# Neighbourhood attention block on one core: the MLP's chain moved over two steps of the band loop, with another order of PSUM bank owners

## The chip, the cores and the metric
One core of one Trainium2 chip. The metric is the device time of one execution, in microseconds (us), median of three runs. Five engines work in parallel, each on its own queue of instructions in program order, and wait for one another through semaphores: TensorE (PE: matrix products into PSUM), VectorE (DVE), ScalarE (ACT), GpSimd (POOL, which works on SBUF alone here) and SyncE (SP, which issues all the DMAs here).

## The reference
The input x is 16 images of 64 x 64 positions with 256 channels, in float32. In short:

```
def norm(x, w, b): return w * arcsinh(x) + b
q, k, v = split(norm(x, n1_w, n1_b) @ qkv_w + qkv_b)        # 8 heads of 32
attn = softmax over the 3 x 3 neighbourhood of (q * 32**-0.5) . k   # clipped at the image's edges
h   = x + (attn . v) @ proj_w + proj_b
out = h + gelu(norm(h, n2_w, n2_b) @ mlp_w1 + mlp_b1) @ mlp_w2 + mlp_b2     # 512 hidden, exact gelu
```

## The kernel before, in words
**Bands.** The image rows are cut into 128 bands (`BANDS`) of 8 rows, 512 tokens each. A band is 8 tiles of 8 x 8 queries, and each tile looks at a 10 x 10 window of keys; rows of marks, added to queries and keys, rule out keys outside the 3 x 3 neighbourhood. Channels lie on partitions. Every product is made in float16 parts: an operand is split in a high part (a rounding, `_hi`) and a low part (the rest, `_lo`), and `three` issues three matmuls, hi x hi, hi x lo and lo x hi. ScalarE mostly makes the high part out of PSUM, VectorE the low part; for the probabilities, the normalised input (`a_parts`), the MLP's input (`b_parts`) and the gelu's output (`g_parts`) GpSimd makes the low part.

**Steps and slots.** The loop runs over steps t = 0 to 129. A step has `SLOTS` = 4 slots k of two tiles, and each engine's `step` function writes out by hand what it issues in which slot. The order of the work is this order; the semaphores only hold it back. On TensorE a slot is: `subtract_max` of its two tiles, `scores` of the next slot, a first product group, `weighted` of the first tile (probabilities x values), a second product group, `weighted` of the second tile, `scores_t` of the next slot's two tiles. In step t the attention is that of band t. The product groups of step t in the kernel before are: slot 0 `turn` (transposes of the second half of band t-1's output), k of band t+2, then the projection of t-1; slot 1 q and v of t+2; slot 2 `mlp_out` of t-2 and `turn` of the first half of t; slot 3 `mlp_in` of t-1.

**Around them.** arcsinh is done as square, log, exp (`root`) and log on ScalarE with `magnitude`, `sum` and `sign` on VectorE: chain 1 for the input of band t+3, chain 2 for h of band t-1. ScalarE's `gelus` loads another activation table before its four gelus and the old one after them (lines 993 and 999). VectorE also takes the maximum of the scores, divides by the sum (`sum_reciprocal`, `normalise`, lines 803 and 812), makes h (`h_from_projection`, 751), adds a bias (`h_plus_bias`, 783) and makes y (`result`, 790).

**PSUM.** Banks 3 to 7 belong to attention (scores 3 and 4, transposed scores 5 and 6, weighted values 7). Banks 0 to 2 are shared by all the products, by the lists at the top (`TURN_BANK`, `K_BANK`, `PROJ_BANK`, `Q_BANK`, `V_BANK`, `OUT_BANK`, `IN_BANK`); before a product overwrites a bank, TensorE waits for the last reader of that bank. `weighted` uses bank 7 for every tile, so it waits for `normalise` of the tile before. In `mlp_in` the first product (bank 2) waits for both y of the band before.

**SyncE.** In step t it issues: `place_queries` (12 copies and the mask's) and `place_keys` (12 copies) for band t+1, SBUF to SBUF; `load_x` of t+4; `store_v` of t+2, which writes the values to a DRAM buffer `v_rows` when both `v_low` are done (2 DMAs); `store_y` of t-2, half 0; `gather_v` of band t+1 (8 DMAs out of `v_rows`, which need the store of t+2 to have landed, since windows reach one row into the next band); `store_y`, half 1.

Lines in the rows: 369 is every TensorE matmul (the helper `mm`), 446 the turns; 989 and 990 the exponentials, 997 the gelu, 911, 915, 920, 929 and 938 the arcsinh chain on ScalarE, 975 `v_high`; 713 the sum, 717 the sign, 771 `v_low`; 1072 p_lo, 1087 and 1089 `b_parts`, 1096 and 1098 `g_parts`; 306 `place_keys`, 314 `store_v`, 325 `gather_v`, 330 `store_y`.

Of the kernel before, what the change touches and what calls it, by code (L numbers as in the profile page):

```python
# [48 lines left out]
XT = 5  # L49
# [11 lines left out]
PROJ_BANK = [0, 1]  # L61
Q_BANK = [2, 0]
V_BANK = [1, 2]
# [39 lines left out]
def build(nc, x, qkv_w, qkv_b, proj_w, proj_b, n1_w, n1_b, n2_w, n2_b, mlp_w1, mlp_b1, mlp_w2, mlp_b2,  # L103
# [3 lines left out]
    with ExitStack() as ctx:  # L107
# [146 lines left out]
        def _(sp):  # L254
# [112 lines left out]
        def _(pe):  # L367
# [11 lines left out]
            def k_product(t, g):  # L379

                if g == 0:
                    pe.wait_ge(a_lo_ready, signals(t, G, G))
                if has(t - 4):
                    pe.wait_ge(gelu_ready, signals(t - 4, MT, 3 + g))
                elif g == 0:
                    pe.wait_ge(v_lo_ready, signals(t - 1, 2, 1))
                    pe.wait_ge(o_lo_ready, signals(t - 3, 2, 1))
                else:
                    pe.wait_ge(v_lo_ready, signals(t - 1, 2, 2))
                k_matmuls(g)  # L390
# [7 lines left out]
            def q_product(t, g):  # L398

                if g == 0:  # L400
                    pe.wait_ge(k_lo_ready, signals(t, G, 2))
                elif has(t - 3):
                    pe.wait_ge(h_ready, signals(t - 3, G, 1))
                else:
                    pe.wait_ge(q_lo_ready, signals(t - 1, G, 2))
# [9 lines left out]
            def v_product(t, n):  # L415

                if n == 1:
                    pe.wait_ge(q_lo_ready, signals(t, G, 1))
                elif has(t - 3):
                    pe.wait_ge(h_ready, signals(t - 3, G, 2))  # L420
# [11 lines left out]
            def turn(t, half):  # L432

                pe.wait_ge(norm_ready, signals(t, TILES, TILES // 2 * (half + 1)))
                if half == 0:
                    if has(t + 2):
                        pe.wait_ge(v_lo_ready, signals(t + 2, 2, 1))
                    else:
                        pe.wait_ge(h_ready, signals(t - 1, G, 2))
                elif has(t - 1):  # L440
                    pe.wait_ge(gelu_ready, signals(t - 1, MT, 2))
# [8 lines left out]
            def projection(t, par, g):  # L450
# [5 lines left out]
                elif has(t - 1):  # L456
                    pe.wait_ge(gelu_ready, signals(t - 1, MT, 3))
# [6 lines left out]
            def mlp_in(t, m):  # L464

                if m == 0 and has(t - 1):
                    pe.wait_ge(y_ready, signals(t - 1, 2, 2))
                elif m == 0:
                    pe.wait_ge(v_lo_ready, signals(t + 3, 2, 2))
                elif m == 1 and has(t - 1):  # L470
                    pe.wait_ge(y_ready, signals(t - 1, 2, 1))
                elif m == 1:
                    pe.wait_ge(q_lo_ready, signals(t + 3, G, 2))
                elif m == 2 and has(t + 1):
                    pe.wait_ge(o_lo_ready, signals(t + 1, 2, 1))
                elif m == 2:
                    pe.wait_ge(h_ready, signals(t, G, 2))
                else:
                    pe.wait_ge(gelu_ready, signals(t, MT, 1))
# [7 lines left out]
            def mlp_out(t, g):  # L487

                if g == 0:
                    pe.wait_ge(g_lo_ready, signals(t, MT, MT))  # L490
                    if has(t + 4):
                        pe.wait_ge(q_lo_ready, signals(t + 4, G, 2))
                    elif has(t + 1):
                        pe.wait_ge(h_ready, signals(t + 1, G, 1))
                    else:
                        pe.wait_ge(gelu_ready, signals(t, MT, 2))
                elif has(t + 4):
                    pe.wait_ge(v_lo_ready, signals(t + 4, 2, 2))
                else:
                    pe.wait_ge(gelu_ready, signals(t, MT, 4))  # L500
                for m in range(MT):
                    s = three(ps[:, OUT_BANK[g], :], [w[:, m, g * P:(g + 1) * P] for w in (w2_hi, w2_lo)],
# [76 lines left out]
            def opening(t):  # L579
# [3 lines left out]
                if t > -3:  # L583
                    pe.wait_ge(a_lo_ready, signals(t + 2, G, G))
                    if t == -1:
                        pe.wait_ge(v_lo_ready, signals(0, 2, 1))
                    k_matmuls(0)
                    if t == -1:
                        pe.wait_ge(v_lo_ready, signals(0, 2, 2))
                    k_matmuls(1)  # L590
                    pe.wait_ge(k_lo_ready, signals(t + 2, G, 2))
                    q_matmuls(0)
                    if t == -1:
                        pe.wait_ge(q_lo_ready, signals(0, G, 2))
                    q_matmuls(1)
                    v_matmuls(0)
                    pe.wait_ge(q_lo_ready, signals(t + 2, G, 1))
                    v_matmuls(1)
# [6 lines left out]
            def step(t, u):  # L605
                par = t % 2
                att, pre, post, fin, fill = has(t), has(t + 2), has(t - 1), has(t - 2), has(t + 3)
                for k in range(SLOTS):
# [28 lines left out]
                    if k == 1 and pre:  # L637
                        v_product(t + 2, 0)
                    if k == 1 and pre:
                        v_product(t + 2, 1)  # L640
                    if k == 2 and fin:
                        mlp_out(t - 2, 1)
                    if k == 2 and att:
                        turn(t, 0)
                    if k == 3 and post:
                        mlp_in(t - 1, 2)
                        mlp_in(t - 1, 3)
# [14 lines left out]
        def _(v):  # L662
# [153 lines left out]
            def opening(t):  # L816
# [10 lines left out]
                else:  # L827
# [5 lines left out]
                    sum1_(t + 3)  # L833
                    q_low(t + 2, t % 2, 0)
                    q_low(t + 2, t % 2, 1)
                    sign1(t + 3, t + 3)
                    v_low(t + 2, 0)
                    v_low(t + 2, 1)
# [3 lines left out]
            def step(t, u):  # L842
                par, old = t % 2, 1 - t % 2
                att, pre, post, fin, fill = has(t), has(t + 2), has(t - 1), has(t - 2), has(t + 3)
                for k in range(SLOTS):
                    ta, ka = (t, k + 1) if k + 1 < SLOTS else (t + 1, 0)
                    more = has(ta)
                    if more:
# [6 lines left out]
                    if k == 1 and pre:  # L855
                        q_low(t + 2, par, 0)
                    if k == 2 and post:
                        sign2(t - 1, old)
                    if k == 2 and fill:
                        magnitude1(t + 3, (u + 3) % XT)  # L860
                    if k == 3 and att:
                        o_low(t, par, 0)
                    if k == 3 and fill:
                        sign1(t + 3, (u + 3) % XT)
                    if k == 3 and post:
                        h_plus_bias(t - 1, old)
# [5 lines left out]
                    if k == 0 and pre:  # L872
                        k_low(t + 2, 1)
# [3 lines left out]
                    if k == 1 and pre:  # L877
                        q_low(t + 2, par, 1)
                    if k == 1 and post:
                        sum2_(t - 1)  # L880
                    if k == 1 and pre:
                        v_low(t + 2, 0)
                    if k == 2 and fill:
                        sum1_(t + 3)
                    if k == 2 and fin:
                        result(t - 2, par, 0)

# [3 lines left out]
                    if k == 0 and post:  # L891
                        magnitude2(t - 1, old)
                    if k == 1 and pre:
                        v_low(t + 2, 1)
                    if k == 2 and fin:
                        result(t - 2, par, 1)
# [9 lines left out]
        def _(act):  # L906
# [94 lines left out]
            def opening(t):  # L1001
# [6 lines left out]
                else:  # L1008
# [5 lines left out]
                    log1_(t + 3)  # L1014
                    q_high(t + 2, t % 2, 0)
# [3 lines left out]
                    v_high(t + 2, 0)  # L1019
                    v_high(t + 2, 1)  # L1020

            def step(t, u):
                par, old = t % 2, 1 - t % 2
                att, pre, post, fill = has(t), has(t + 2), has(t - 1), has(t + 3)
                for k in range(SLOTS):
# [4 lines left out]
                    if k == 2 and post:  # L1030
                        log2_(t - 1)
# [4 lines left out]
                    if k == 0 and pre:  # L1036
                        k_high(t + 2, 0)
                        k_high(t + 2, 1)
                        windows_main(t + 2, par, 0)
                        windows_main(t + 2, par, 1)  # L1040
                    if k == 1 and pre:
                        q_high(t + 2, par, 0)
                    if k == 1 and post:
                        square2(t - 1, old)
                    if k == 1 and pre:
                        q_high(t + 2, par, 1)
                    if k == 1 and post:
                        log_of_square(ln2_s[:], sq2, ln2a, t - 1)
                        root(ln2_s[:], ln2a, root2, t - 1)
                    if k == 1 and pre:  # L1050
                        v_high(t + 2, 0)
                        v_high(t + 2, 1)
                    if k == 2 and fill:
# [3 lines left out]
                        log1_(t + 3)  # L1057
                    if k == 3 and post:
                        gelus(t - 1)
# [7 lines left out]
        def _(pool):  # L1067
# [56 lines left out]
            def step(t, u):  # L1124
                par, old = t % 2, 1 - t % 2
                att, pre, post, fin, fill = has(t), has(t + 2), has(t - 1), has(t - 2), has(t + 3)
                for k in range(SLOTS):
# [3 lines left out]
                    if k == 0 and fin:  # L1131
                        g_parts(t - 2, (0, 1))
# [35 lines left out]
```

## Time and profile before
| | |
|---|---|
| time, median of 3 runs | 4478.32 us (4474.22 to 4479.34) |
| profiled execution | 4478.71 us, span 4476.9 us |
| busy: PE / DVE / ACT / POOL | 4089.1 (91%) / 3570.1 (80%) / 3663.0 (82%) / 3539.3 (79%) |
| PE waits for y of `result` (DVE L790) | 283.3 us in 126 waits |
| mean granted TensorE clock | 0.969 of full speed |
| DMA engines busy | about half the time, 134 GB/s |

A busy PE is not a PE at its peak: matmuls overlap, and the start of one to the start of the next tells the pace. Waits are put down to the work that released them. The clock is granted at one of two levels, so a mean of 0.969 means short stretches at half speed.

### The profile page before, as it was taken

To read this page: it belongs to the slowest core of one execution; us is meant where nothing else is said; L and a number is where in the kernel's file an instruction comes from. 1 tells how busy PE (TensorE), PEld (TensorE's weight loads), DVE (VectorE), ACT (ScalarE), POOL (GpSimd) and SP (SyncE) were. 2 spreads that over 40 slices of the span, in tenths; PEclk is the share of its full clock that TensorE was granted. 3 is DMA by queue.
4 is the path that set the end of the run, shared out by engine and by line. 5 is a ranking of instruction groups with operands and counts; after the bars stand their busy time and mean duration, and the time that the engine had idled before them with its cause. 6 is when DMAs were issued, how large, how long until landed. Compare 5 with 4: busy or idle time off the path is not lost.

```text
span 4476.9 us, 123492 instructions
## 1 busy us (share of the span) xinstructions
PE 4089.1 (91%) x47688; PEld 2566.3 (57%) x47688; DVE 3570.1 (80%) x6174; ACT 3663.0 (82%) x5377; POOL 3539.3 (79%) x4092
## 2 busy tenths in 40 slices
PE   5999999999999999999999999999999999999997
PEld 3555555555555555555555555555555555555553
DVE  5788788888878888887888888788878888887884
ACT  4888888888888888888888888888888888888884
POOL 2788888887888888888878888888888788788885
PEclk8999999999999999999999999999999999999998
DMA  4555555555555555555555555555555555555551
GB/s 121 129 142 134 136 135 138 138 134 137 138 135 134 141 137 132 142 134 138 133 140 138 133 136 139 136 133 142 133 137 135 138 138 133 137 138 136 134 133 55
DMA packets 511560, 598.82 MB, mean 134 GB/s; under 512 B 76798, under 2 KB 409600, under 8 KB 508416
## 3 DMA queue, kind: packets, MB, share of 16 engines
q1 hardware_dynamic: 510976, 590.93, 51.2%
q8 instruction: 379, 6.21, 0.6%
q14 instruction: 205, 1.68, 0.1%
HBM read 197.30 MB, written 135.40 MB: 74 GB/s over the span
## 4 chain that ended last, share of the span: by engine, by line
PE 51%; DVE 23%; issue 14%; ACT 10%; POOL 1%; SPq 1%; DMA 0%; DVEq 0%; POOLq 0%; ACTq 0%
PE ps L369 49%; DVE ln_u L717 4%; DVE y L790 4%; DVE v_nat L771 4%; DVE o_norm L812 3%; DVE ln_u L713 3%; ACT ln_s L920 3%; ACT ln_s L911 3%; ACT ln_s L915 3%; DVE ln_u L710 2%; ACT q_nat L944 2%; PE ps L446 2%; DVE maxima L796 2%; DVE recip L803 1%; POOL g_lo L1098 0%
## 5 line engine op out<-in xcount | busy, mean ns | idle before, releaser
L1072 POOL TENSOR_TENSOR p_lo<-prob,p_hi 100x512 f16<-100x512 f32 x1024 | 1312.7, 1287 | 623.7 <-ACT p_hi L990 623.5
L369 PE MATMUL ps<-b_hi,w_hi 128*128 128x512 f16 x1024 | 435.7, 425 | 288.4 <-DVE y L790 283.3
L989 ACT ACTIVATE prob<-ps 100x512 f32<-100x512 f32 x1024 | 610.2, 596 | 80.2 <-PE ps L369 54.9
L713 DVE TENSOR_TENSOR ln_u<-ln_u,ln_s 128x1024 f32<-128x1024 f32 x256 | 531.0, 2074 | 147.2 <-ACT ln_s L920 143.4
L812 DVE TENSOR_TENSOR o_norm<-ps,recip 64x128 f32<-64x128 f32 x2048 | 591.7, 289 | 49.4
L1098 POOL TENSOR_TENSOR g_lo<-g,g_hi 128x512 f16<-128x512 f32 x512 | 594.9, 1162 | 41.0
L369 PEld LDWEIGHTS ps<-v_win,p_hi 100*128 100x128 f16 x8192 | 474.7, 98 | 261.3 <-DVE o_norm L812 70.7
L990 ACT ACTIVATE p_hi<-ps 100x512 f16<-100x512 f32 x1024 | 613.7, 599 | 0.0
L796 DVE TENSOR_REDUCE maxima<-ps 128x8 bf16<-128x800 f32 x512 | 504.6, 986 | 88.3 <-PE ps L369 84.2
L369 PE MATMUL ps<-v_win,p_hi 100*128 100x65 f16 x8192 | 517.5, 194 | 47.7 <-DVE o_norm L812 26.4
L997 ACT ACTIVATE g<-ps,b 128x512 f32<-128x512 f32 x512 | 344.6, 686 | 254.5 <-PE ps L369 253.6
L369 PE MATMUL ps<-v_win,p_lo 100*128 100x65 f16 x4096 | 481.6, 192 | 0.0
L1087 POOL CAST b_hi<-ln_u 128x512 f16<-128x512 f32 x256 | 329.3, 1286 | 150.2 <-DVE ln_u L717 150.2
L369 PE MATMUL ps<-b_lo,w_hi 128*128 128x512 f16 x1024 | 432.4, 422 | 0.0
L369 PE MATMUL ps<-b_hi,w_lo 128*128 128x512 f16 x1024 | 421.2, 411 | 0.0
L929 ACT ACTIVATE ln_s<-ln_u 128x1024 f32<-128x1024 f32 x128 | 135.3, 1057 | 332.4 <-DVE ln_u L713 332.4
L369 PE MATMUL ps<-a_hi,wqkv_hi 128*128 128x512 f16 x1024 | 391.8, 383 | 13.3 <-DVE bp L705 6.3
L369 PE MATMUL ps<-g_hi,w_hi 128*128 128x512 f16 x1024 | 392.4, 383 | 8.3 <-POOL g_lo L1098 8.3
L966 ACT ACTIVATE k_win<-k_nat 128x640 f16<-128x640 f16 x512 | 349.4, 730 | 51.7 <-DVE k_nat L764 47.7
L369 PE MATMUL ps<-g_lo,w_hi 128*128 128x512 f16 x1024 | 390.6, 381 | 0.0
L369 PE MATMUL ps<-g_hi,w_lo 128*128 128x512 f16 x1024 | 390.4, 381 | 0.0
L369 PE MATMUL ps<-a_lo,wqkv_hi 128*128 128x512 f16 x1024 | 390.3, 381 | 0.0
(91 smaller groups left out, 10887.7 us busy)
## 6 DMA issues: line engine op xcount, KB each, us to landing
keys<-k_win SPq DMA_DIRECT2D x1536, 100.0 KB, 2.2
v_win<-v_rows SPq DMA_DIRECT2D x1024, 101.6 KB
queries<-q_nat SPq DMA_DIRECT2D x1536, 64.0 KB
v_rows<-v_nat SPq DMA_DIRECT2D x256, 260.0 KB, 5.4
xT<-in_x_dram SPq DMA_DIRECT2D x128, 512.0 KB, 4.3
out_dram<-y SPq DMA_DIRECT2D x256, 256.0 KB, 2.7
queries<-in_query_mask_dram SPq DMA_DIRECT2D x128, 160.0 KB
keys<-in_mlp_w_dram SPq DMA_DIRECT2D x2, 512.0 KB, 7.7
```

The source lines that it names most:

```text
L369: return pe.matmul(o, a, b, start=start, stop=stop, skip_group_check=True)
L713: v.tensor_tensor(u, u, root, ALU.add).then_inc(s, 1)
L717: v.scalar_tensor_tensor(out=out.bitcast(U32), in0=sign_of.bitcast(U32), scalar=SIGN, in1=log.bitcast(U32), op0=ALU.bitwise_and, op1=ALU.b ...
L796: v.tensor_reduce(maxima[k % 2][:].rearrange("p n a -> p (n a)"), ps[:, B_S:B_S + 2, 0:PAIRS * NK].rearrange("p n (a k) -> p n a k", k=NK) ...
L812: s = v.tensor_tensor(o_norm[r, c], av[r, :, HD * e:HD * e + HD], recip[c % 2][r].to_broadcast([NQ, PAIRS, HD]), ALU.mult)
L966: s = act.activation(to[:, :, 1:1 + TS], rows, ACT.Copy)
L989: act.activation(prob[b][0:NK], ps[0:NK, B_ST + b, :], ACT.Exp, scale=INV * INV).then_inc(prob_ready, 1)
L990: act.activation(p_hi[b][0:NK], ps[0:NK, B_ST + b, :], ACT.Exp, scale=INV * INV).then_inc(p_hi_ready, 1)
L997: act.activation(g32[:, m, :], ps[:, IN_BANK[m], :], ACT.Gelu, bias=b1[:, m:m + 1], scale=INV).then_inc(gelu_ready, 1)
L1072: pool.tensor_tensor(p_lo[b][0:NK], prob[b][0:NK], p_hi[b][0:NK], ALU.subtract).then_inc(p_lo_ready, 1)
L1087: pool.tensor_copy(b_hi[:, g, :], ln2_u[:, g * TOK:(g + 1) * TOK]).then_inc(b_hi_ready, 1)
L1098: pool.tensor_tensor(g_lo[:, m, :], g32[:, m, :], g_hi[:, m, :], ALU.subtract).then_inc(g_lo_ready, 1)
```

## The change
The MLP's first product moves from the last slot of one step to slot 1 of the next, so that in step t both `mlp_in` and `mlp_out` are those of band t-2; with it move `sign2`, `b_parts`, `gelus` and `h_plus_bias`. q and v change slots (both in slot 2, v first), `mlp_out` goes to slot 3, and V's banks become 0 and 1. The square and the roots of both arcsinh chains are placed anew. On SyncE `store_y` of half 0 goes behind `gather_v`. `mlp_out` waits for the four parts of g one by one. The same instructions are issued per band. The core of the diff:

```
-V_BANK = [1, 2]
+V_BANK = [0, 1]
@@ SyncE step
-                if has(t - 2):
-                    store_y(t - 2, 0)
                 if has(t + 1):
                     gather_v(t + 1, 1 - par)
                 if has(t - 2):
+                    store_y(t - 2, 0)
                     store_y(t - 2, 1)
@@ TensorE: k_product
                 if g == 0:
                     pe.wait_ge(a_lo_ready, signals(t, G, G))
-                if has(t - 4):
-                    pe.wait_ge(gelu_ready, signals(t - 4, MT, 3 + g))
...
+                    if has(t - 3):
+                        pe.wait_ge(o_lo_ready, signals(t - 3, 2, 1))
...
+                elif has(t - 5):
+                    pe.wait_ge(y_ready, signals(t - 5, 2, 2))
@@ q_product
-                if g == 0:
-                    pe.wait_ge(k_lo_ready, signals(t, G, 2))
-                elif has(t - 3):
-                    pe.wait_ge(h_ready, signals(t - 3, G, 1))
+                if g == 1:
+                    pe.wait_ge(v_lo_ready, signals(t, 2, 1))
+                elif has(t - 4):
+                    pe.wait_ge(gelu_ready, signals(t - 4, MT, 4))
@@ v_product
-                if n == 1:
-                    pe.wait_ge(q_lo_ready, signals(t, G, 1))
+                if has(t - 4):
+                    pe.wait_ge(gelu_ready, signals(t - 4, MT, 2 + n))
@@ turn
-                        pe.wait_ge(v_lo_ready, signals(t + 2, 2, 1))
+                        pe.wait_ge(v_lo_ready, signals(t + 2, 2, 2))
...
-                elif has(t - 1):
-                    pe.wait_ge(gelu_ready, signals(t - 1, MT, 2))
+                elif has(t - 2):
+                    pe.wait_ge(y_ready, signals(t - 2, 2, 1))
@@ mlp_in
-                if m == 0 and has(t - 1):
-                    pe.wait_ge(y_ready, signals(t - 1, 2, 2))
...
+                if m == 0:
+                    if has(t + 4):
+                        pe.wait_ge(k_lo_ready, signals(t + 4, G, 2))
...
+                elif m == 3:
+                    pe.wait_ge(gelu_ready, signals(t, MT, 1))
+                elif has(t + 1):
+                    pe.wait_ge(h_ready, signals(t + 1, G, m))
@@ mlp_out
-                if g == 0:
-                    pe.wait_ge(g_lo_ready, signals(t, MT, MT))
...
                 for m in range(MT):
+                    if g == 0:
+                        pe.wait_ge(g_lo_ready, signals(t, MT, m + 1))
@@ TensorE step, first product groups (before weighted of tile 2k)
-                    if k == 1 and pre:
-                        q_product(t + 2, 0)
-                        q_product(t + 2, 1)
-                    if k == 2 and fin:
+                    if k == 1 and fin:
+                        mlp_in(t - 2, 0)
+                        mlp_in(t - 2, 1)
+                    if k == 2 and pre:
+                        v_product(t + 2, 0)
+                        v_product(t + 2, 1)
+                    if k == 3 and fin:
                         mlp_out(t - 2, 0)
-                    if k == 3 and post:
-                        mlp_in(t - 1, 0)
-                        mlp_in(t - 1, 1)
@@ second groups: mlp_in 2 and 3 in slot 1, q 0 and 1 in slot 2, mlp_out 1 in slot 3
@@ VectorE: h_from_projection
+                if g == 0 and has(t - 2):
+                    v.wait_ge(y_ready, signals(t - 2, 2, 2))
@@ GpSimd: a_parts, step
-                pool.wait_ge(pe_v, signals(t - 1, 2, 2))
+                pool.wait_ge(pe_q, signals(t - 1, G, G))
...
                     if k == 0 and fin:
-                        g_parts(t - 2, (0, 1))
+                        b_parts(t - 2)
...
                     if k == 1 and fin:
+                        g_parts(t - 2, (0, 1))
+                    if k == 2 and fin:
                         g_parts(t - 2, (2, 3))
-                    if k == 2 and post:
-                        b_parts(t - 1)
```

The steps of VectorE and ScalarE after the change, slot by slot (rn is `sum_reciprocal` and `normalise` of a tile, pp the two exponentials of a tile):

```
VectorE  k=0: sign2(t-2), maximum, o_low(t-1,1), k_low x2, rn, magnitude1(t+3), h_from_projection x2, rn
         k=1: maximum, sum1_(t+3), magnitude2(t-1), rn, h_plus_bias(t-2), rn
         k=2: maximum, sign1(t+3), v_low x2, rn, q_low x2, rn
         k=3: maximum, o_low(t,0), sum2_(t-1), rn, result(t-2) x2, rn
ScalarE  k=0: pp, o_high(t-1,1), pp, k_high x2, square1, log, root of t+3
         k=1: pp, pp, gelus(t-2)
         k=2: pp, log1_(t+3), pp, v_high x2, square2(t-1), q_high x2, log of the square
         k=3: pp, o_high(t,0), pp, root of t-1, windows_main x2 (t+2), log2_(t-1)
```

## Rows read from the trace of the kernel before

**Rows 1.** The profile's page, part 1: busy time and share of each engine.
```profile
PE 4089.1 (91%) x47688; PEld 2566.3 (57%) x47688; DVE 3570.1 (80%) x6174; ACT 3663.0 (82%) x5377; POOL 3539.3 (79%) x4092
```

**Rows 2.** Waits of TensorE, whole run: total us, times, longest.
```profile
PE ps L369 <- DVE y L790: 283.3, 126, 2.3
...
PE ps L369 <- DVE o_norm L812: 26.4, 126, 3.2
```

**Rows 3.** Timeline of TensorE, two bands: start, us, work, [idle before].
```profile
2249.32 0.61 PE L369 MATMUL ps<-b_hi,w_hi 128*128 128x512 f16 x1 [2.29 <-DVE y L790]
...
2257.35 0.61 PE L369 MATMUL ps<-minus_ident,maxima 128*128 128x128 bf16 x8
...
2261.45 0.23 PE L369 MATMUL ps<-v_win,p_hi 100*128 100x65 f16 x2
...
2265.24 0.61 PE L369 MATMUL ps<-minus_ident,maxima 128*128 128x128 bf16 x8
...
2268.86 0.23 PE L369 MATMUL ps<-v_win,p_hi 100*128 100x65 f16 x2
...
2271.86 0.23 PE L369 MATMUL ps<-v_win,p_hi 100*128 100x65 f16 x2
...
2272.69 0.61 PE L369 MATMUL ps<-minus_ident,maxima 128*128 128x128 bf16 x8
...
2284.27 0.39 PE L369 MATMUL ps<-b_hi,w_hi 128*128 128x512 f16 x1 [2.29 <-DVE y L790]
...
2317.59 0.61 PE L369 MATMUL ps<-b_hi,w_hi 128*128 128x512 f16 x1 [2.29 <-DVE y L790]
```

**Rows 4.** Table by windows: clock behind the wait at 2249.32.
```profile
2249.32:2252.73 3.41, 3.40 (x9) 1.23 (x10) 3.41 (x4) 3.16 (x5) 3.10 (x2) 0.51 0.41 104
```

**Rows 5.** Timeline of ScalarE: table load, exponentials, `v_high`.
```profile
2257.41 1.28 ACT L999 ACT_TABLE_LOAD   x1
...
2271.92 1.07 ACT L975 ACTIVATE v_nat<-ps 128x512 f16<-128x512 f32 x2
...
2275.28 0.58 ACT L989 ACTIVATE prob<-ps 100x512 f32<-100x512 f32 x1
...
2276.23 1.06 ACT L911 ACTIVATE ln_s<-xT 128x1024 f32<-128x1024 f32 x1
```

**Rows 6.** Groups by line: the costs of VectorE's and GpSimd's steps.
```profile
L713 DVE TENSOR_TENSOR ln_u<-ln_u,ln_s 128x1024 f32<-128x1024 f32 x256 | 531.0, 2074 | 147.2 <-ACT ln_s L920 143.4
...
L1072 POOL TENSOR_TENSOR p_lo<-prob,p_hi 100x512 f16<-100x512 f32 x1024 | 1312.7, 1287 | 623.7 <-ACT p_hi L990 623.5
...
L1087 POOL CAST b_hi<-ln_u 128x512 f16<-128x512 f32 x256 | 329.3, 1286 | 150.2 <-DVE ln_u L717 150.2
...
L771 DVE SCALAR_TENSOR_TENSOR v_nat<-ps,v_nat 128x512 f16<-128x512 f32 x256 | 175.6, 687 | 6.5 <-ACT v_nat L975 2.6
```

**Rows 7.** Timeline of SyncE's queue in the opening steps: gather, store.
```profile
70.30 6.46 SPq L325 DMA_DIRECT2D v_win<-v_rows  x8
...
95.19 0.98 SPq L314 DMA_DIRECT2D v_rows<-v_nat  x2
...
101.22 6.42 SPq L325 DMA_DIRECT2D v_win<-v_rows  x8
...
131.41 6.41 SPq L325 DMA_DIRECT2D v_win<-v_rows  x8
```

**Rows 8.** Timeline of SyncE's queue, steady state: `store_y`, `gather_v`.
```profile
2316.12 0.35 SPq L330 DMA_DIRECT2D out_dram<-y  x1
...
2316.58 6.77 SPq L325 DMA_DIRECT2D v_win<-v_rows  x8
```

**Rows 9.** Timeline of TensorE, opening: `weighted` released by the gather at 70.30.
```profile
79.16 0.29 PE L369 MATMUL ps<-v_win,p_hi 100*128 100x65 f16 x2 [5.03 <-DMA v_win<-v_rows]
```

**Rows 10.** The page, part 6: DMA issues, KB, us to landing.
```profile
v_rows<-v_nat SPq DMA_DIRECT2D x256, 260.0 KB, 5.4
...
out_dram<-y SPq DMA_DIRECT2D x256, 256.0 KB, 2.7
```

More of the change, by code:

```diff
@@ L636, in step @@
                         projection(t - 1, 1 - par, 1)
[L637 to L642, printed above, removed]
+                    if k == 1 and fin:
+                        mlp_in(t - 2, 2)
+                        mlp_in(t - 2, 3)
+                    if k == 2 and pre:
+                        q_product(t + 2, 0)
+                        q_product(t + 2, 1)
                     if k == 2 and att:
                         turn(t, 0)
[L645 to L647 removed]
+                    if k == 3 and fin:
+                        mlp_out(t - 2, 1)
                     if att:
@@ L847, in step @@
                     more = has(ta)
+                    if k == 0 and fin:
+                        sign2(t - 2, par)
                     if more:
@@ L854, in step @@
                         k_low(t + 2, 0)
-                    if k == 1 and pre:
-                        q_low(t + 2, par, 0)
-                    if k == 2 and post:
-                        sign2(t - 1, old)
+                        k_low(t + 2, 1)
+                    if k == 1 and fill:
+                        sum1_(t + 3)
+                    if k == 1 and post:
+                        magnitude2(t - 1, old)
                     if k == 2 and fill:
-                        magnitude1(t + 3, (u + 3) % XT)
+                        sign1(t + 3, (u + 3) % XT)
+                    if k == 2 and pre:
+                        v_low(t + 2, 0)
+                        v_low(t + 2, 1)
                     if k == 3 and att:
                         o_low(t, par, 0)
-                    if k == 3 and fill:
-                        sign1(t + 3, (u + 3) % XT)
                     if k == 3 and post:
-                        h_plus_bias(t - 1, old)
+                        sum2_(t - 1)
                     if att:
@@ L876, in step @@
                         h_from_projection(t - 1, old, (u - 1) % XT, 1)
-                    if k == 1 and pre:
+                    if k == 1 and fin:
+                        h_plus_bias(t - 2, par)
+                    if k == 2 and pre:
+                        q_low(t + 2, par, 0)
                         q_low(t + 2, par, 1)
[L879 to L885, printed above, removed]
+                    if k == 3 and fin:
                         result(t - 2, par, 0)
+                        result(t - 2, par, 1)
                     if att:
@@ L890, in step @@
                         normalise(t, 2 * k + 1)
[L891 to L896, printed above, removed]
             for t_ in queries:
@@ L1038, in step @@
                         k_high(t + 2, 1)
[L1039 to L1053, printed above, removed]
+                    if k == 0 and fill:
                         square1(t + 3, (u + 3) % XT)
@@ L1056, in step @@
                         root(ln1_s[:], ln1a, root1, t + 3)
-                        log1_(t + 3)
-                    if k == 3 and post:
-                        gelus(t - 1)
+                    if k == 1 and fin:
+                        gelus(t - 2)
+                    if k == 2 and pre:
+                        v_high(t + 2, 0)
+                        v_high(t + 2, 1)
+                    if k == 2 and post:
+                        square2(t - 1, old)
+                    if k == 2 and pre:
+                        q_high(t + 2, par, 0)
+                        q_high(t + 2, par, 1)
+                    if k == 2 and post:
+                        log_of_square(ln2_s[:], sq2, ln2a, t - 1)
+                    if k == 3 and post:
+                        root(ln2_s[:], ln2a, root2, t - 1)
+                    if k == 3 and pre:
+                        windows_main(t + 2, par, 0)
+                        windows_main(t + 2, par, 1)
+                    if k == 3 and post:
+                        log2_(t - 1)
             for t in range(-3, 0):
```

82 lines of the change are left out of this document (34 added, 48 removed).

## The prediction
> **What bounds the kernel now.** I read the page's busy times first [rows 1]: TensorE 91%, the other three engines about 80%. Divided by 128 bands that is 27.9 us a band for VectorE, 28.6 for ScalarE and 27.7 for GpSimd. The band's length stands in TensorE's timeline [rows 3]: the product `mlp_in` starts after the same wait at 2249.32, 2284.27 and 2317.59, so two bands are 68.27 us and one is 34.13. Three engines thus have 5.5 to 6.5 us to spare, and TensorE is the one to follow. Its waits [rows 2] are of one kind: 126 times on `result` (y), 283.3 us in all or 2.25 a band, and 126 times on `normalise` (o_norm), 0.2 a band. A second loss goes with the first: matmuls last 0.61 us after the wait at 2249.32 and at 2317.59, but 0.39 after that at 2284.27 [rows 3], and the granted clock of the 3.41 us behind the first is 0.51 of full speed, its 1.2 GHz level [rows 4]. The band with that stretch is 34.95 us, the one without it 33.32, so the level costs 1.6 us in every other band, 0.8 a band. What TensorE did ahead of each fall was to wait 2.29 us; after one such wait of two it did not fall.
>
> TensorE without either loss: 33.32 - 2.25 - 0.2 = 30.87 us a band. That is the floor. Its slots [rows 3], counted from `subtract_max` of slot 0 at 2257.35 as s0: s1 = s0 + 7.89, s2 = s0 + 15.34. `weighted` of the first tile of slot 0 comes at s0 + 4.10, of another slot at s + 3.62 (2268.86), of the second tile at s + 6.62 (2271.86). The four products of each slot have the same length after the change, as each slot still holds two groups of 12 passes of 512 columns (or 24 of 256), and the turns stay in slots 0 and 2, so these offsets can be kept.
>
> **What goes.** `mlp_in`'s first product waited for both results of the band before, because banks 2 and 0 were OUT banks until `result` had read them. It now comes in slot 1, and `result` in slot 3, so between `mlp_out` and the next owners of its banks (k's second product and the turn, slot 0) lies the end of a step. I cost the y wait at 0 and its slow stretches at 0. No matmul, activation, copy or DMA is added or taken away in a steady band; only the order changes, so the question is what is late next. I went round each engine's queue at the floor's offsets.
>
> **ScalarE and TensorE, slot 2.** The gelus move to slot 1. Before, the table load behind the last gelu runs from 2257.41 to 2258.69, s0 + 1.34 [rows 5]; after `mlp_in`'s last product at the same place of slot 1 this gives s2 + 1.34. A pair of exponentials takes 0.95 (2275.28 to 2276.23), GpSimd's p_lo 1.29 on the mean [rows 6], and `weighted` can start at s2 + 3.7 with the latencies, against 3.62: a stall of 0.1 (in slot 0 the turn hid this). From there ScalarE does the pair (0.95), log1 (128x1024 like the square at 2276.23, 1.06, the next start 1.0 later), a second pair (0.95) and two `v_high` (1.07), then VectorE the second `v_low`, 0.69 [rows 5, 6]: 1.34 + 0.95 + 1.0 + 0.95 + 1.07 + 0.1 + 0.69 = s2 + 6.1 to 6.3. I take 6.2. q's second product, whose bank 0 is now v's first, waits for the first `v_low` at about s2 + 5.6 where it would start at 5.3 to 5.4: 0.2.
>
> **VectorE, slot 3.** `root2` stands behind all four exponentials and `o_high`, so it ends near s3 + 0.6 + 0.95 + 0.5 + 0.95 + 1.07 = 4.1; `sum2_` needs it and lasts 2.07 [rows 6], to 6.2; reciprocal and `normalise` of the slot's first tile stand behind it, to 7.0. `weighted` of the slot's second tile wants that bank at 6.62: 0.4 to 0.5. With 0.1 and 0.2 of slot 2, TensorE alone would run a band in 30.87 + 0.8 = 31.6 us. If `sum2_` or ScalarE were half a us faster there, the third stall would go and it would be 31.2.
>
> **GpSimd.** `b_parts` moves to slot 0, behind two p_lo and VectorE's `sign2`, which now opens the step. Casts of b average 1.29 us, a subtraction like p_lo 1.29 at most [rows 6]; with some overlap two of each are about 4.9, from about s0 + 4.7 to 9.6, against need at s1 + 1.0 for the first half (ready by then, as it is half of the work) and s1 + 1.7 = s0 + 9.6 for the second. Cost 0, up to 0.3 if the casts stay slow. Behind it stand `windows_bottom` and then p_lo of slot 1, whose `weighted` has about 0.2 of slack; same bounds. `h_plus_bias`, `magnitude2` and the a parts keep over 0.5 us of slack in their slots. The new wait of `h_from_projection` for y of two bands back is for something done a slot earlier: 0.
>
> **SyncE's queue.** This is what I think decides. `store_v` waits for `v_low` of both halves, which moves from slot 1 and 2 to s2 + 6.2; before, the store left at 2276.6, s2 + 4, and SyncE then waited for y with time over. `gather_v` waits until that store has landed, and `weighted` of the next step's slot 0 waits for the gather. The chain [rows 7 to 9]: from the store's start at 95.19 to the gather's at 101.22 are 6.03 us, when nothing but the landing was between; from a gather's start at 70.30 to the `weighted` released by it at 79.16 are 8.86 us. Together 14.89. From there TensorE needs 2272.69 - 2261.45 = 11.24 us to the start of slot 2, and 6.2 to `v_low`. The circle closes in 14.89 + 11.24 + 6.2 = 32.3 us, over TensorE's 31.6. `store_y` of half 0 moves behind the gather, which keeps y out of this circle; its issue is 0.35 us [rows 8].
>
> SyncE's queue by itself is a circle too. Gather to gather in the opening steps, without y stores, is 131.41 - 101.22 = 30.19 us [rows 7]; two y stores with gaps (0.35 and about 0.5) make 31.1, and the steady state's longer issues (a gather 6.77 in row 8 against 6.46 in rows 7) some 31.3 to 31.7.
>
> The landing is the unknown term. The v store shows 5.4 us, behind the x load issued just before it, a y store of the same 256 KB that stands alone 2.7 [rows 10]. If the 5.4 is the queue behind x, then SyncE's wait for `v_low` (0.6 us at a band of 32.3) is taken off it, and the circle is 31.7; if not, 32.3. At the row of y it would be 29.6 and bind nothing. I take 32.1, near the upper end, as x is still directly in front.
>
> The Trainium skill (DMA: Bandwidth & Descriptors, "Anatomy of one DMA", the SWDGE path) says that a DMA's fixed cost is about 2.0 us, most of it the wait until the last byte is confirmed, and that the rest is bytes over 436 GB/s. For 260 KB this would be an estimated 2.6 us, near the y row's 2.7 and half of the store's 5.4; by that rule the chain through the store is no bound, and the time is that of rival A.
>
> **Sum.** The wait is met 126 times, so 126 x (34.13 - 32.1) = 256 us go. The ends: the last band's MLP now runs wholly in the last step behind its arsinh, while its gelus of the band before precede it on ScalarE; `mlp_out` starts as soon as the first quarter of g is split. I put +3 us (bounds -5 and +10). Profiled time 4478.7 - 256 + 3 = 4226. The median of the runs before is 4478.3, the same.
>
> **Rivals.**
> A: the store lands sooner, and TensorE's small stalls or SyncE's issue circle set the band at 31.2 to 31.7. For it: the y row's 2.7 us; against: x in front. 126 x 2.6 = 330 us less: 4150. Chance 0.22.
> B: the clock still falls in every other band, now after the waits at `weighted` and in slot 3. For it: the level fell after 2.29 us of waiting; against: each new wait is under 1 us. Price 0.8 a band: 4330. Chance 0.15.
> C: a wait of the same 2 us replaces the old one, GpSimd's chain in slot 0 and 1 being a microsecond later than I have it: no change, 4475 or so. Against it: 6.4 us of spare time a band there. With other partial losses between 4370 and 4470, chance 0.10.
> D, slower: the wait for `v_win` drops the clock each band rather than each second one. Everything from `weighted` in slot 0 to slot 2 is on the circle, so a 3.4 us stretch at half speed adds 1.7 us to 32.3, and two in a row 3.4: 35.7 a band, 4478.7 + 126 x 1.57 = 4677. It turns to slower once the clock costs more than 2.0 us a band. Against: it cost 0.8 with a wait of 2.3. Chance 0.06.
>
> **Chances and range.** Forecast, 4190 to 4290: 0.47. The range takes in A and B: 4130 to 4370. No change within 0.2% (9 us, about what a measurement here can tell) is a small part of C, 0.03; slower is D with a little of C, 0.08; faster 0.89.
>
> **What would show it.** Right: no wait on y; a band of 32.1; TensorE waiting 0.3 to 1 us on v_win once a band, 0.1 to 0.5 on o_norm in slot 3; `store_v` directly behind `v_low` with SyncE idle before it; hardly any half clock. Wrong: v_win not in the waits (A); PEclk still near 0.97 (B); a wait over 1 us on p_lo or b_lo (C). A store that lands after about 5.4 us again confirms that term; one near 3 breaks it.

## The result, and the profile after

The changed kernel takes 4221.46 us (median of 4 runs, 4218.82 to 4228.25) against 4478.4 us; the ratio is 0.943 with a 95% interval of 0.9414 to 0.9447. The forecast was 4226. The profiled execution took 4228.25 us, its span is 4226.5.

The page of the changed kernel, parts 1 and 4 (the chain that ended last, by engine and by line; TensorE's line is now 368):

```profile
PE 4022.6 (95%) x47688; PEld 2518.8 (60%) x47688; DVE 3637.2 (86%) x6174; ACT 3630.9 (86%) x5377; POOL 3636.9 (86%) x4092
...
PE 46%; SPq 18%; DMA 14%; POOL 9%; issue 7%; ACT 4%; DVE 2%; POOLq 0%; ACTq 0%; DVEq 0%
PE ps L368 46%; SPq L325 14%; DMA v_win<-v_rows 8%; DMA v_rows<-v_nat 6%; POOL p_lo L1065 3%; POOL g_lo L1091 2%; SPq L306 2%; DVE v_nat L766 1%; SPq L292 1%; POOL g_hi L1089 1%; POOL a_lo L1073 1%; ACT ln_s L920 1%; POOL a_hi L1071 1%; ACT p_hi L981 1%; ACT v_nat L966 1%
```

TensorE is busy 95% of the span, and the chain that ended last now runs through SyncE's issues (SPq 18%) and through DMAs in flight (14%). The same line of the kernel before:

```profile
PE 51%; DVE 23%; issue 14%; ACT 10%; POOL 1%; SPq 1%; DMA 0%; DVEq 0%; POOLq 0%; ACTq 0%
```

TensorE's waits over the whole run (total us, times, longest) answer to [rows 2]:

```profile
PE ps L368 <- DMA v_win<-v_rows: 114.3, 109, 5.7
PE ps L368 <- POOL p_lo L1065: 25.5, 25, 2.7
...
PE ps L368 <- DVE o_norm L807: 7.8, 6, 2.7
```

The wait on y (283.3 us in 126 times) is gone altogether, and 114.3 us on v_win, 0.9 a band, stand in its place. The wait on o_norm in slot 3, forecast at 0.4 to 0.5 us a band, isn't there: 7.8 us in 6 waits, all outside the steady part.

The band's length is read from SyncE's queue (start, us, work): a gather near the loop's start and the 124th after it (the first row shows two of its eight DMAs),

```profile
133.36 1.69 SPq L325 DMA_DIRECT2D v_win<-v_rows  x2
...
4113.28 6.44 SPq L325 DMA_DIRECT2D v_win<-v_rows  x8
```

3979.92 us for 124 bands, 32.10 us each; the forecast was 32.1. The kernel before, from 131.41 [rows 7] to this gather, has 34.12 over as many:

```profile
4362.10 6.44 SPq L325 DMA_DIRECT2D v_win<-v_rows  x8
```

Outside of these bands, the kernel before had 246 us in its span and this one has 247, so the ends cost about nothing (forecast +3).

The same table by windows as [rows 4], over the same 340 us of both kernels, some ten bands (the column behind the busy times is the granted clock). Before:

```profile
2000.00:2340.00 340.00, 315.36 (x3688) 197.62 (x3686) 276.66 (x480) 284.68 (x418) 275.83 (x320) 0.97 0.53 137
```

After:

```profile
2000.00:2340.00 340.00, 331.00 (x3969) 206.85 (x3967) 301.63 (x512) 301.88 (x448) 304.80 (x345) 1.00 0.55 146
```

The clock is at its 2.4 GHz level throughout this stretch, 1.00 against 0.97. TensorE's timeline over one band after, with the same landmarks as [rows 3] (`subtract_max` of slots 0 to 3 and 0, and the wait at `weighted` of slot 0):

```profile
2263.23 0.61 PE L368 MATMUL ps<-minus_ident,maxima 128*128 128x128 bf16 x8
...
2269.01 0.23 PE L368 MATMUL ps<-v_win,p_hi 100*128 100x65 f16 x2 [1.52 <-DMA v_win<-v_rows]
...
2272.81 0.61 PE L368 MATMUL ps<-minus_ident,maxima 128*128 128x128 bf16 x8
...
2280.23 0.61 PE L368 MATMUL ps<-minus_ident,maxima 128*128 128x128 bf16 x8
...
2288.45 0.61 PE L368 MATMUL ps<-minus_ident,maxima 128*128 128x128 bf16 x8
...
2295.87 0.61 PE L368 MATMUL ps<-minus_ident,maxima 128*128 128x128 bf16 x8
```

Slots 1 and 3 are 7.42 us long, slot 2 8.22, and slot 0 is 9.58, of which 1.52 is the wait for v_win. In the stretch of that table 9 of 11 bands have this wait, of 0.2 to 1.6 us. Slot 2 of the kernel before went from 2272.69 [rows 3] to 2280.89 with 0.17 of waiting in it, 8.03 without; so 0.2 us is new, and q's second product, which waits for the first `v_low`, is where it lies (e6 below, with an earlier `v_low`, has 8.06).

SyncE's queue over one round. The last row is the first of the eight DMAs of the next gather:

```profile
2259.92 6.43 SPq L325 DMA_DIRECT2D v_win<-v_rows  x8
2266.39 0.95 SPq L330 DMA_DIRECT2D out_dram<-y  x2
2267.45 8.01 SPq L292 DMA_DIRECT2D queries<-q_nat  x12
2275.50 0.52 SPq L295 DMA_DIRECT2D queries<-in_query_mask_dram  x1
2276.11 8.50 SPq L306 DMA_DIRECT2D keys<-k_win  x12
2284.66 0.59 SPq L276 DMA_DIRECT2D xT<-in_x_dram  x1
2286.45 0.93 SPq L314 DMA_DIRECT2D v_rows<-v_nat  x2
2291.30 0.85 SPq L325 DMA_DIRECT2D v_win<-v_rows  x1
```

Nothing lies between the issues from 2259.92 to 2285.25; then SyncE waits 1.2 us for `v_low`, issues the store, and waits 3.9 us from the end of its issue for the landing (the time until a DMA's last byte is reported to be in place; the page counts it from the issue). Whole run, SyncE's waits:

```profile
SPq L320 <- DMA v_rows<-v_nat: 557.0, 127, 6.3
SPq L314 <- DVE v_nat L766: 123.8, 110, 8.2
```

and the landing, from the page's part 6: 

```profile
v_rows<-v_nat SPq DMA_DIRECT2D x256, 260.0 KB, 4.5
```

4.5 us against 5.4 in [rows 10]: where SyncE waits for `v_low` first, the landing is shorter by about as much. That was the open question of the forecast, and the experiments were chosen for it.

### The profile page after: what moved, and what is told of

Same layout as the page of the kernel before. It is cut to its first block, busy times and chain, and to the rows that moved or that the text cites. A ratio compares the mean times of both kernels' runs of the same rounds, so it can differ in the third digit from the quotient of the medians.

```text
span 4226.5 us, 123614 instructions
## 1 busy us (share of the span) xinstructions
PE 4022.6 (95%) x47688; PEld 2518.8 (60%) x47688; DVE 3637.2 (86%) x6174; ACT 3630.9 (86%) x5377; POOL 3636.9 (86%) x4092
## 4 chain that ended last, share of the span: by engine, by line
PE 46%; SPq 18%; DMA 14%; POOL 9%; issue 7%; ACT 4%; DVE 2%; POOLq 0%; ACTq 0%; DVEq 0%
PE ps L368 46%; SPq L325 14%; DMA v_win<-v_rows 8%; DMA v_rows<-v_nat 6%; POOL p_lo L1065 3%; POOL g_lo L1091 2%; SPq L306 2%; DVE v_nat L766 1%; SPq L292 1%; POOL g_hi L1089 1%; POOL a_lo L1073 1%; ACT ln_s L920 1%; POOL a_hi L1071 1%; ACT p_hi L981 1%; ACT v_nat L966 1%
## 5 line engine op out<-in xcount | busy, mean ns | idle before, releaser
L368 PEld LDWEIGHTS ps<-v_win,p_hi 100*128 100x128 f16 x8192 | 464.6, 98 | 396.9 <-DMA v_win<-v_rows 185.6
L368 PE MATMUL ps<-v_win,p_hi 100*128 100x65 f16 x8192 | 516.8, 194 | 150.3 <-DMA v_win<-v_rows 114.3
L706 DVE TENSOR_TENSOR ln_u<-ln_u,ln_s 128x1024 f32<-128x1024 f32 x256 | 367.5, 1435 | 162.5 <-ACT ln_s L911 158.7
L368 PE MATMUL ps<-b_hi,w_hi 128*128 128x512 f16 x1024 | 390.7, 382 | 5.0 <-POOL b_lo L1082 5.0
L1089 POOL CAST g_hi<-g 128x512 f16<-128x512 f32 x512 | 360.2, 704 | 38.7 <-ACT g L988 38.3
L368 PE MATMUL ps<-a_hi,wqkv_lo 128*128 128x512 f16 x1024 | 389.7, 381 | 0.0
L368 PE MATMUL ps<-b_hi,w_lo 128*128 128x512 f16 x1024 | 389.0, 380 | 0.0
L368 PE MATMUL ps<-b_lo,w_hi 128*128 128x512 f16 x1024 | 388.9, 380 | 0.0
L368 PEld LDWEIGHTS ps<-v_win,p_lo 100*128 100x128 f16 x4096 | 382.9, 96 | 0.0
```

The source lines that it names most:

```text
L368: return pe.matmul(o, a, b, start=start, stop=stop, skip_group_check=True)
L706: v.tensor_tensor(u, u, root, ALU.add).then_inc(s, 1)
L1089: pool.tensor_copy(g_hi[:, m, :], g32[:, m, :]).then_inc(g_hi_ready, 1)
```

## The experiments

Two theories had the same sum. V: the circle through `v_low`, the store, its landing, the gather and `weighted` sets the band, `v_low` being part of it at all times. S: SyncE's own queue is the circle, from gather to gather, and the landing counts from the x load in front of the store, so that `v_low` may come up to a microsecond late unseen. Rival P: TensorE's own order sets the band. Each run was timed beside the kernel before on the same chip.

| run | us | ratio to before (95%) | band against the changed kernel |
|---|---|---|---|
| changed kernel | 4221.5 | 0.943 (0.9414 to 0.9447) | |
| e1, y store of half 0 first | 4913.4 | 1.097 (1.0953 to 1.0986) | +5.5 |
| e2, v store before x load | 4176.6 | 0.9326 (0.9312 to 0.934) | -0.36 |
| e3, v_high before log1 | 4224.5 | 0.9436 (0.9422 to 0.945) | 0 |
| e4, gather of old rows | 4128.5 | 0.9217 (0.9202 to 0.9233) | -0.74 |
| e5, kernel before, SyncE's edit alone | 4478.8 | 1.0001 (0.9992 to 1.001) | |
| e6, e2 and e3 together | 4114.6 | 0.9189 (0.9176 to 0.9203) | -0.85 |
| e7, without the mask's DMA | 4157.8 | 0.929 (0.9273 to 0.9306) | -0.51 |
| e8, y stores from ScalarE's queue | 4146.7 | 0.9264 (0.9248 to 0.9279) | -0.59 |
| e9, e6 and e8 together | 4115.5 | 0.9189 (0.9174 to 0.9204) | -0.84 |
| e10, one DMA more a band | 4272.4 | 0.953 (0.9507 to 0.9552) | +0.40 |

The last column is the difference to 4221.5 over 126 bands. The kernel before had medians of 4478.0 to 4478.9 in all these sets of runs, so times of different sets can be set side by side.

**e1: the SyncE edit undone.**

```
                 if has(t - 2):
                     store_y(t - 2, 0)
                 if has(t + 1):
                     gather_v(t + 1, 1 - par)
                 if has(t - 2):
                     store_y(t - 2, 1)
```

> Theory V (the circle v_low, v store, landing, gather, weighted of the next slot 0 sets the changed kernel's band at 31.9 us): y of half 0 is done some 6.7 us into slot 3 and the gather now starts 3 to 4 us into it, so with that y store ahead of it the gather starts 3.5 us later in each band and the band becomes about 35.4 us: 4221 + 126 x 3.5 = 4660, slower than the kernel before, with TensorE waiting 4 to 5 us a band on v_win. Rival P (TensorE's own order and small stalls set the band, the wait for v_win is a by-product of a few tenths): under 4260. Rival C (the time came from the clock alone): 4221.

The direction is right and rivals P and C fall, but 4913 is 250 us more than forecast. Its wait for v_win in the whole run, and its clock over 340 us, nine bands:

```profile
PE ps L369 <- DMA v_win<-v_rows: 602.9, 127, 7.2
```

```profile
2000.00:2340.00 340.00, 297.19 (x3370) 181.81 (x3371) 255.00 (x437) 257.29 (x384) 253.60 (x290) 0.95 0.47 125
```

The wait is 4.7 us a band, within the 4 to 5 that I had given it; what I had left out is the clock, which with waits of that length is 0.95. Its price is read from the slots (`subtract_max` of slot 1, of the next slot 0 and of the slot 1 after it, with the wait):

```profile
2250.89 0.61 PE L369 MATMUL ps<-minus_ident,maxima 128*128 128x128 bf16 x8
...
2273.95 0.61 PE L369 MATMUL ps<-minus_ident,maxima 128*128 128x128 bf16 x8
...
2283.28 0.24 PE L369 MATMUL ps<-v_win,p_hi 100*128 100x65 f16 x2 [5.06 <-DMA v_win<-v_rows]
...
2288.74 0.61 PE L369 MATMUL ps<-minus_ident,maxima 128*128 128x128 bf16 x8
```

Slots 1 to 3 take 23.06 us together, as in the changed kernel. Slot 0 is 14.79 us, 9.73 without the wait, against 8.06 there (9.58 - 1.52), so 1.7 us longer. The 5.46 us behind the wait have a granted clock of 0.69, which accounts for it (0.31 x 5.46 = 1.7):

```profile
2283.28:2288.74 5.46, 5.46 (x52) 2.97 (x53) 2.84 (x6) 0.00 (x0) 0.42 (x3) 0.69 0.44 111
```

Times 126 that is about 210 of the 250 us. What the other 40 are is open. So without the two moved lines this change would be 10% slower than the kernel before.

**e5: the same two lines in the kernel before.**

> The kernel before with SyncE's edit alone (store_y of half 0 behind the gather). There the band is set by the circle through y (TensorE's 2.25 us wait a band), which this edit does not touch, and the gather has time over: 4478, no change. If the SyncE edit by itself carried part of the gain, it is below 4465.

4478.8 us. The SyncE edit earns nothing alone, and the rest of the change loses without it: neither part has a gain of its own that could be added.

**e4: the circle cut.**

```
-                sp.wait_ge(v_out, signals(t + 1, 16 * V_DMAS, 16 * V_DMAS if has(t + 1) else 0))
-                rows = v_rows[bass.ds(t * TOK, 2 * PAD_ROWS + TOK)]
+                src = max(t - 2, 0) if isinstance(t, int) else t - 2
+                sp.wait_ge(v_out, signals(src + 1, 16 * V_DMAS, 16 * V_DMAS))
+                rows = v_rows[bass.ds(src * TOK, 2 * PAD_ROWS + TOK)]
```

> The gather reads the rows of the band two before (long landed) in place of its own, so it waits for no fresh store; the values are those of another band, all instructions and bytes are the same. Theory V: the circle is cut, no wait on v_win, TensorE at 30.87 plus the 0.3 of slot 2: 31.2 us a band, 4221 - 126 x 0.75 = 4127. Rival P: 4221, another wait of TensorE's takes its place. This is the whole price of the circle.

4128.5 us: with the circle cut the band is 0.74 us shorter, as the floor and slot 2's stall gave it. P falls. In the waits small ones on p_lo are left:

```profile
PE ps L369 <- POOL p_lo L1066: 39.3, 131, 2.7
```

**e3: `v_low` a microsecond earlier.**

```
 ScalarE  k=2: pp, [log1_ taken away] pp, v_high x2, log1_(t + 3), square2, ...
 VectorE  k=2: maximum, v_low x2, rn, sign1(t + 3), q_low x2, rn
```

> log1 goes behind v_high on ScalarE and sign1 behind v_low on VectorE, nothing else. Theory V: v_low is done 1.0 us earlier in slot 2, SyncE's wait for it (1.1 us a band) goes, the circle shortens by 0.7 to 1.0 until TensorE's 31.2 or SyncE's own queue (31.3 to 31.7) binds: 4130 to 4180. Rival P: 4221 or, if the later sign1 delays rn, a little above.

4224.5 us, no change: theory V as I had it is wrong. SyncE's waits and the landing show why:

```profile
SPq L320 <- DMA v_rows<-v_nat: 618.1, 127, 6.6
...
SPq L314 <- DVE v_nat L766: 61.5, 57, 7.2
```

```profile
v_rows<-v_nat SPq DMA_DIRECT2D x256, 260.0 KB, 5.2
```

The wait for `v_low` fell from 123.8 to 61.5 us and the wait for the landing rose from 557.0 to 618.1, by 62 and 61 us. The landing went from 4.5 to 5.2 us. One round of this run, with the store directly behind x:

```profile
2184.74 0.60 SPq L276 DMA_DIRECT2D xT<-in_x_dram  x1
2185.38 0.99 SPq L314 DMA_DIRECT2D v_rows<-v_nat  x2
2191.73 6.78 SPq L325 DMA_DIRECT2D v_win<-v_rows  x8
```

From the store to the gather are 6.35 us where the changed kernel's round had 4.85, from x's issue to the gather 6.99 and 6.64. On the mean of 120 steady bands x's issue to the gather is 7.00 us here and 6.94 in the changed kernel, while the store's distance behind x went from 1.51 to 0.98. So the gather comes at a fixed time after x's issue, within limits: in the changed kernel's bands whose store left less than 1.7 us behind x it was 6.7 us on the mean (70 bands), in the others 7.3 (50 bands).

**e2: the store in front of the x load.**

```
+                if has(t + 2):
+                    store_v(t + 2)
                 if t >= 0 and has(t + 4):
                     if has(t - 1):
                         sp.wait_ge(h_ready, signals(t - 1, G, G))
                     load_x(t + 4)
-                if has(t + 2):
-                    store_v(t + 2)
```

> Only SyncE's order of the x load and the v store is swapped. Theory V, with the store's landing (4.4 us after its issue where SyncE had waited, 5.4 in the kernel before) being mostly the queue behind the 512 KB of x: landing near 3, the circle is 1.5 us shorter, TensorE falls to its floor of 31.2 us a band: about 4130, no waits on v_win. If the landing is the confirmation of a write to HBM and not the queue: landing stays above 4, 4200 to 4221. Rival P: 4221.

Half of what was expected, 45 us, between the two values that were named. The landing is 4.2 us and not 3, so what is left of it is not x in front; and `v_low` now does bind, since nothing covers it:

```profile
SPq L320 <- DMA v_rows<-v_nat: 423.6, 127, 4.1
SPq L314 <- DVE v_nat L766: 209.6, 127, 8.0
```

SyncE waits 209.6 us for it in 127 times, so in every band.

**e6: both.** 

> The changed kernel with the v store ahead of the x load and v_high ahead of log1 together. Each alone gave 4177 and 4224. Theory S (SyncE's own queue is the circle: gather, y, queries, keys, x, store and its landing, and v_low's time is only hidden behind the landing that x's bytes prolong): with the store in front of x the landing counts from v_low, so now the earlier v_low pays: about 31.2 us a band, 4130 to 4145. Theory V as it stood (v_low in the circle at all times) says the same here but not 4224 for v_high alone. If neither: 4177.

4114.6 us, 15 below the forecast of S. v_high ahead of log1, which gave 0 on the changed kernel, gives 62 us once the store stands in front of x. S says both; V says a gain in both places. TensorE's waits of the whole run, and its windows row:

```profile
PE ps L368 <- POOL p_lo L1065: 15.0, 8, 2.7
PE ps L368 <- DMA v_win<-v_rows: 15.0, 14, 4.7
```

```profile
2000.00:2340.00 340.00, 337.35 (x4065) 213.01 (x4064) 308.74 (x523) 307.44 (x458) 320.07 (x349) 1.00 0.57 149
```

PE is busy 337.35 of 340 us and hardly waits for v_win; this is the floor of its order. Its slot 2 (`subtract_max` of slots 2 and 3) takes 8.06 us where the changed kernel's took 8.22, as the first `v_low` comes earlier:

```profile
2242.85 0.61 PE L368 MATMUL ps<-minus_ident,maxima 128*128 128x128 bf16 x8
...
2250.91 0.61 PE L368 MATMUL ps<-minus_ident,maxima 128*128 128x128 bf16 x8
```

**e7 and e10: one issue less, one issue more.**

```
 e7:  the copy of query_mask_c only for t < 2
 e10: + sp.dma_start(queries[par][P - spare:P]..., query_mask_c[b][0:spare]).then_inc(q_in[par], 16)
```

> The changed kernel without the mask's DMA in place_queries after the first two bands (the mask is left as those bands had it, so part of the masking is wrong): 0.62 us less of SyncE's issue a band and 160 KB less traffic. Theory S: the issue circle is 0.6 us shorter, until v_low binds: 31.4 us a band, 4150. Theory V (v_low binds): 4221, as the wait for v_low takes up the time.

> The changed kernel with one DMA more in each place_queries (96 KB of the mask into 12 partitions that nothing reads), the opposite of the run without the mask. Theory S (SyncE's queue of issues is the circle): some 0.6 us more a band, 4221 + 126 x 0.55 = 4290. If v_low binds, it is hidden in SyncE's wait of 1 us for v_low: 4221 to 4235.

4157.8 and 4272.4 us, -0.51 and +0.40 us a band. Both lie on S's side; e10 costs less than the 0.55 forecast, since the added DMA took less time to issue than I had given it:

```profile
2004.12 0.33 SPq L298 DMA_DIRECT2D queries<-in_query_mask_dram  x1
```

SyncE's timeline splits each band in two, from the gather's start to x's issue, and from there over the store and its landing to the next gather (us, means of 120 steady bands):

| run | gather to x | x to gather | band |
|---|---|---|---|
| changed kernel | 25.15 | 6.94 | 32.09 |
| e3, v_high before log1 | 25.16 | 7.00 | 32.15 |
| e7, without the mask's DMA | 24.57 | 7.05 | 31.62 |
| e8, y stores from ScalarE's queue | 24.23 | 7.22 | 31.45 |
| e10, one DMA more | 25.54 | 6.98 | 32.52 |

What an edit does to the band it does in the first part, which is issues alone. The second part, where the DMA traffic would show, does not get shorter with 160 KB less (e7) and hardly longer with 96 KB more (e10). It grows by 0.1 and 0.3 where x is issued earlier (e7, e8) and the store, which waits for `v_low`, is left further behind it: there the circle through `v_low` takes over in some of the bands.

**e8: the y stores on ScalarE's queue.**

```
+                    if k == 0 and has(t - 3):
+                        store_y(t - 3, 0)      # act.wait_ge, act.dma_start
+                        store_y(t - 3, 1)
```

> The changed kernel with both y stores issued from ScalarE's queue in slot 0 of the next step: 1.06 us less of SyncE's issue a band, at the price of two issues on ScalarE, which has 4 us to spare a band but is tight in slot 0. Theory S: the circle is about 1 us shorter until v_low or TensorE's floor binds, 4130 to 4160. Theory V: 4221. If an issue costs ScalarE over 0.5 us each in slot 0: above 4221.

4146.7 us (the cut shows the added part; SyncE's two `store_y` are taken away): the bytes are the same, the queue that issues them is another, and 0.59 us a band go. The y bytes also move at another time of the band, so the time alone does not prove that it is the issue; the table's first part does, with 0.92 us less, of which the second gives 0.28 back. SyncE now waits longer for `v_low`, 253.5 us against 123.8:

```profile
SPq L314 <- DVE v_nat L758: 253.5, 126, 8.6
```

**e9: all three.** 

> v store ahead of x, v_high ahead of log1, and both y stores on ScalarE's queue together. The first two gave 4115 with TensorE waiting for v_win only 15 us in all, so it stands on TensorE's floor (31.1 us a band). Theory S: taking issue time off SyncE buys nothing more, 4105 to 4118; the two issues on ScalarE can cost a few us through p_lo, up to 4130. Below 4095 would mean that the floor was not TensorE's order.

4115.5 us, the same as e6 within their intervals: on TensorE's floor, SyncE's time is worth nothing. e6 is the faster version of this kernel to keep, 2.5% under the changed kernel.

## Why the prediction was right, point by point

**What goes.** Right: no wait on y, no slow stretch. The 2.25 us, the 0.8 us of clock and the 0.2 on o_norm a band all went, 3.25, and 0.9 on v_win, 0.2 in slot 2 and 0.1 to 0.2 in slot 0 came back: 34.12 - 32.10 = 2.02 us a band, against 2.03 forecast.

**TensorE's floor.** Right: 30.87 and slot 2's forecast 0.3 make 31.2. e4, with neither v_win nor y to wait for, is (4221.5 - 4128.5) / 126 = 0.74 under 32.10, so 31.36, with about 0.2 of waits for p_lo in it; e6 is 0.85 under, 31.25.

**Slot 2.** Nearly right: 0.2 measured, 0.3 (0.1 and 0.2) forecast. `v_low` was done at s2 + 6.2: the slot began at 2280.23, the store left at 2286.45.

**Slot 3.** Wrong: `sum2_` was to last 2.07 us and to make `weighted` wait 0.4 to 0.5. VectorE's group by line for the sums and, on GpSimd, for the cast of a, in the changed kernel:

```profile
L706 DVE TENSOR_TENSOR ln_u<-ln_u,ln_s 128x1024 f32<-128x1024 f32 x256 | 367.5, 1435 | 162.5 <-ACT ln_s L911 158.7
...
L1071 POOL CAST a_hi<-ln_u 128x512 f16<-128x512 f32 x256 | 279.0, 1090 | 44.4 <-DVE ln_u L710 44.4
```

the cast in the kernel before:

```profile
L1078 POOL CAST a_hi<-ln_u 128x512 f16<-128x512 f32 x256 | 179.7, 702 | 45.3 <-DVE ln_u L717 45.3
```

and the one sum of slot 3 in the band shown above, from VectorE's timeline:

```profile
2259.85 1.27 DVE L706 TENSOR_TENSOR ln_u<-ln_u,ln_s 128x1024 f32<-128x1024 f32 x1 [1.18 <-ACT ln_s L911]
```

The sum's mean fell from 2074 ns [rows 6] to 1435; in slot 3 it is 1.27. The prediction had named this case (`sum2_` half a us faster, and the stall goes) and had no row to choose it by. It didn't matter to the time, because the band of 32.1 was set elsewhere.

**GpSimd.** Right: b was ready in time, and the p_lo waits are 25.5 us in 25 times, 0.2 a band.

**SyncE.** The total came out and the circle that I put in front was the wrong one; that 32.1 was met is in part luck. I had the circle through `v_low` at 32.3, or 31.7 if the landing was x's queue, and SyncE's own at 31.3 to 31.7, and took 32.1 between the two values of the first. The band is 32.10, but e3 shows that an earlier `v_low` gives nothing, and e7, e8 and e10 that issue time in SyncE's queue does. The one round shown above has 25.33 us of issues, 1.2 of waiting for `v_low` and 4.85 from the store's start to the next gather, 31.4; the mean is 32.09. So the term at fault is SyncE's own circle, 0.4 to 0.8 too short. I had read it from the kernel before's opening steps, where x was issued at

```profile
124.66 0.60 SPq L276 DMA_DIRECT2D xT<-in_x_dram  x1
```

which is 23.44 us behind the gather at 101.22 [rows 7], 24.3 with the 0.85 of the y stores; in the steady part of the changed kernel it is 25.15. From x to the gather it was 6.75 there and is 6.94 now. The landing's lower value, with the wait for `v_low` taken off it, was the true one: its 5.4 us should have been counted from x's issue. That put the first circle too high and left the second too low, and the two errors cancelled.

**The rule of the Trainium skill** (DMA: Bandwidth & Descriptors, "Anatomy of one DMA", about 2.0 us fixed and the bytes on top, an estimated 2.6) does not hold for this store. The page gives it for DMAs issued from GpSimd, and these are SyncE's. With x behind it and not in front the store still took 4.2 us (e2). In e1 it left 3.8 us behind x's issue (2260.68 and 2264.52), when x, whose landing is 3.8 there, was about through, and took

```profile
v_rows<-v_nat SPq DMA_DIRECT2D x256, 260.0 KB, 3.6
```

so 1.0 us over the rule is left with nothing just in front. The measurement decides; what fills that 1.0 was not tried.

**The rivals.** A (4150) was where e2, e7 and e8 went, not this kernel. B: the clock did not fall (0.991 on the mean of the run, 0.969 before). D: its mechanism, a wait for v_win that drops the clock, is what e1 showed once the wait is 4.7 us instead of 0.9.

## What to carry to other kernels

When a stall is taken out of the engine that leads, go round every queue for the next circle, the DMA-issuing one included: here SyncE, whose issues the profile's page does not count as busy, became the bound. A DMA's landing read from the trace is partly the queue in front of it; to know whether an earlier producer pays, move the producer and look whether the issuing engine's wait for it and its wait for the landing add up to the same as before (681 and 680 us here). And an edit that earns nothing alone (e5, e3) can be what another edit stands on (e1, e6).

## What the runs showed of the hardware

An addition of two float32 SBUF operands of 128 x 1024 on VectorE took 1.27 us in slot 3 of the changed kernel and 2.07 on the mean before, with no change to the instruction. Over the same two runs GpSimd's cast of a went from 702 ns to 1090 on the mean. That the reason is what the other engine runs beside each is a guess; it was not tried.

TensorE's clock kept its 2.4 GHz level (1.00 over 340 us, some ten bands) with waits of 0.2 to 1.6 us at one place of a 32 us band, and had a mean of 0.95 with waits of 4.7 us there (e1); before, with a wait of 2.29 us in each band, it fell behind two of the three in [rows 3].

A store of 260 KB to DRAM, issued by SyncE, landed in 5.2 us directly behind a load of 512 KB (e3), 4.5 us some 1.5 us behind it (changed kernel), 4.2 us in front of it (e2) and 3.6 us when the load was about through (e1).
